# One pair of VectorE operations makes the block exponents of two tiles of h instead of one

## The chip, the cores and the metric

The kernel runs on one core of a Trainium2 chip. The metric is the device time in microseconds (us), from the first to the last instruction and what lies around them; the profile's span covers the instructions alone. Three runs of the kernel before have a median of 321.7 us (321.41 to 323.46).

## The reference

A post-norm transformer block on x of shape [2, 2048, 256]: linear attention, then an MLP whose two linear layers take block-quantised operands.

```
x = layernorm(x + attn(x))        # q, k, v = x Wqkv^T + b, scaled; q, k -> elu + 1
                                  # y = q * cumsum(k v) / clip(sum(q * cumsum(k)), 1e-3); y Wproj^T + b
x = layernorm(x + ffn(x))         # h = gelu(bq(x) bq(w_fc)^T + b_fc); bq(h) bq(w_proj)^T + b_proj

bq(v): in each block of 32 along the last axis
    e = floor(log2(max |v|));  scale = 2^(e - 3);  q = round(v / scale) * scale
```

The hidden layer h has 1024 columns, so each token has 32 blocks, each with a power of two of its own.

## The kernel before

**Tiling.** The 4096 tokens are cut into 8 chunks of 512; the chunks of the two sequences alternate. A chunk is 4 tiles of 128 tokens (tokens on the partitions), t = 0 to 3. Of a chunk the attention, the first layer norm, the up projection with gelu (h, four tiles of [128, 1024]), the quantisation of h, the down projection and the second layer norm are computed.

**Staging.** A step of the loop works on three chunks at once: A has its attention begun, B its attention ended, its first norm made and its up projection begun, and C has the rest of its MLP done. There is a written-out start, then 6 steps (a loop of 3 rounds, two steps in each), then a written-out tail for chunks 6 and 7. Each engine has a queue that it works through strictly in the order of the program text; the order of `step` in each engine's block sets the order of work. Engines wait for each other by semaphore counts; a waiting instruction holds up all that stands behind it on its engine.

**Quantising a tile of h.** Six operations on three engines:
1. VectorE takes the maximum of each block (`h_exponents`, line 718, `h_amax`), once both gelu halves of the tile are there (`s_h`).
2. VectorE masks the exponent bits of the maxima, which is the power of two (`powers`, line 621, `h_pow`).
3. VectorE makes the grid factor from it (`powers`, line 624, `h_inv`) and counts `s_hinv`.
4. GpSimd multiplies h with the factor into float16, which rounds (`round_h`, line 326, `h_round`; `h_round` has two buffers).
5. VectorE multiplies back with the power (`quantise_h`, line 629 in `times_power`, `hq`).
6. TensorE transposes `hq` (`transpose_hq`, line 957), ScalarE copies it from PSUM (`copy_hT`, line 446), TensorE does the down projection (`down`, line 964), VectorE adds the residual (`residual_2`, line 730).

The same `powers` serves the weights (lines 633 to 640) and x (`x_exponents`, line 706).

**Orders around the change.** VectorE's `step` ends with `h_exponents(B, 0)`, two `attention_out` (line 682, `y`), `h_exponents(B, 1)`, `quantise_h(B, 0)`. The next step, in which this chunk is C, begins with `h_exponents(C, 2)`, `residual_1(B, 0)` (line 686, `r1`), `quantise_h(C, 1)`, `h_exponents(C, 3)`, `residual_1(B, 1)`, `mean_var_1(B)`. GpSimd's `step` ends with `round_h(B, 0)`, `round_h(B, 1)`; the next begins with `round_h(C, 2)`, `scale_shift_1(B)` (lines 311 and 313), `round_h(C, 3)`. TensorE's has, in this order, `transpose_rec` (line 919), `up(C, 2)`, `project_out(B, 0)` (line 932), `up(C, 3)`, `transpose_hq(C, 0)`, `project(A)` for k (line 900), `project_out(B, 1)`, `project(A)` for q, `down(C, 0)`.

In the tail, VectorE does `mean_var_1(7)`, `h_exponents(6, 2)`, `quantise_h(6, 1)`, `x_exponents(7)`, `quantise_h(6, 2)`, `residual_2(6, 0)`, `quantise_x(7)`, `residual_2(6, 1)`, `h_exponents(6, 3)`. TensorE can start `up(6, 3)` only after `transpose_hq(6, 1)` and `down(6, 0)`; ScalarE does `norm_1(7)`, `copy_hT(6, 1)` and then the gelu of (6, 3) at line 436. GpSimd's tail is `scale_shift_1(7)`, `round_h(6, 2)`, `round_x(7)` (line 317), `round_h(6, 3)`, `round_h(7, 0)`, `round_h(7, 1)`, `round_h(7, 2)`, `scale_shift_2(6)`, `round_h(7, 3)`, `scale_shift_2(7)`. ScalarE's `norm_2(6)` (line 455, `o_sb`) stands before `copy_hT(7, 1)`, and VectorE's `residual_2(7, 0)` waits for it.

Of the kernel before, what the change touches and what calls it, by code (L numbers as in the profile page):

```python
# [45 lines left out]
def wait(engine, sem, value):  # L46

    if isinstance(value, int) and value <= 0:
        return
    engine.wait_ge(sem, value)  # L50


def block_kernel(nc, x, Wqkv, bqkv, Wproj, bproj, scale, w_fc, b_fc, w_pr, b_pr, out):
# [3 lines left out]
    TILES = 4  # L57
# [4 lines left out]
    HC = HID // P  # L62
# [3 lines left out]
    XB = C // BLOCK_K  # L66
    HB = HID // BLOCK_K
# [7 lines left out]
    with ExitStack() as ctx:  # L75
        def sb(name, shape, dt=F32):
            return ctx.enter_context(nc.sbuf_tensor(name, shape, dt))
# [4 lines left out]
        def sem(name):  # L82
            return ctx.enter_context(nc.semaphore(name))
# [13 lines left out]
        w_amax = sb("w_amax", [P, 2, HC * XB])  # L97
        w_inv = sb("w_inv", [P, 2, HC * XB], BF16)
        w_pow = sb("w_pow", [P, 2, HC * XB, 2], BF16)
# [36 lines left out]
        x_amax = sb("x_amax", [P, TILES * XB])  # L136
        x_inv = sb("x_inv", [P, TILES * XB], BF16)
        x_pow = sb("x_pow", [P, TILES * XB, 2], BF16)
# [6 lines left out]
        h_amax = sb("h_amax", [P, TILES, HB])  # L145
        h_inv = sb("h_inv", [P, TILES, HB], BF16)
        h_pow = sb("h_pow", [P, TILES, HB, 2], BF16)
# [38 lines left out]
        s_w_amax, s_w_exp, s_w_inv, s_w_round, s_wq = sem("w_amax_done"), sem("w_exponent_done"), sem("w_grid_ready"), sem("w_rounded"), sem("w_quantised")  # L186
# [31 lines left out]
        s_xamax, s_xexp, s_xinv = sem("x_amax_done"), sem("x_exponent_done"), sem("x_grid_ready")  # L218
# [6 lines left out]
        s_hamax, s_hexp, s_hinv = sem("h_amax_done"), sem("h_exponent_done"), sem("h_grid_ready")  # L225
# [65 lines left out]
        def _(pool):  # L291
# [28 lines left out]
                                        ALU.mult).then_inc(s_xround, 1)  # L320

            def round_h(S, t):
                wait(pool, s_hinv, 4 * S + t + 1)
                if t >= 2:
                    wait(pool, s_hq, 4 * S + t - 1)
                nc.gpsimd.tensor_tensor(h_round[:, t % 2].rearrange("p (g j) -> p g j", j=BLOCK_K),  # L326
                                        h[:, t].rearrange("p (g j) -> p g j", j=BLOCK_K),
                                        h_inv[:, t].unsqueeze(2).broadcast_to([P, HB, BLOCK_K]),
                                        ALU.mult).then_inc(s_hround, 1)
# [258 lines left out]
        def _(dve):  # L588
# [25 lines left out]
                        dve.wait_ge(s_bsplit, 2 * r + 2)  # L614
                    src = b_rest

            def powers(amax, pow2, inv, groups, s_amax, s_pow, s_inv, n):

                top = amax.bitcast(U16).rearrange("p (g o) -> p g o", o=2)[:, :, 1:2]
                wait(dve, s_amax, n)  # L620
                nc.vector.tensor_scalar(pow2.bitcast(U16), top.broadcast_to([P, groups, 2]), EXPONENT_BITS, None,  # L621
                                        ALU.bitwise_and).then_inc(s_pow, 1)
                wait(dve, s_pow, n)
                nc.vector.tensor_scalar(inv.bitcast(U16), pow2.bitcast(U16)[:, :, 0], -1.0, float(TO_GRID),  # L624
                                        ALU.mult, ALU.add).then_inc(s_inv, 1)

            def times_power(dst, src, pow2, groups):
                pairs = BLOCK_K // 2
                return nc.vector.tensor_tensor(dst.rearrange("p (g j o) -> p g j o", j=pairs, o=2),  # L629
                                               src.rearrange("p (g j o) -> p g j o", j=pairs, o=2),  # L630
                                               pow2.unsqueeze(2).broadcast_to([P, groups, pairs, 2]), ALU.mult)

            def w_exponents(n):
                w, w_sem = ((w_fc_sb, s_wfc), (w_pr_sb, s_wpr))[n]
                w = w.rearrange("p e (g j) -> p (e g) j", j=BLOCK_K)
                dve.wait_ge(w_sem, 16)
                nc.vector.tensor_reduce(w_amax[:, n], w, AX_X, ALU.max, apply_absolute_value=True).then_inc(s_w_amax, 1)
                powers(w_amax[:, n], w_pow[:, n], w_inv[:, n], HC * XB, s_w_amax, s_w_exp, s_w_inv, n + 1)
                dve.wait_ge(s_w_inv, n + 1)
                nc.vector.tensor_scalar(w_pow[:, n], w_pow[:, n], PRODUCT_STEP, None, ALU.mult).then_inc(s_w_pow, 1)  # L640

# [64 lines left out]
            def x_exponents(S, b):  # L706
                wait(dve, s_x1, S + 1)
                nc.vector.tensor_reduce(x_amax[:, :], x1[:, b].rearrange("p t (g j) -> p (t g) j", j=BLOCK_K), AX_X,  # L708
                                        ALU.max, apply_absolute_value=True).then_inc(s_xamax, 1)
                powers(x_amax[:, :], x_pow[:, :, :], x_inv[:, :], TILES * XB, s_xamax, s_xexp, s_xinv, S + 1)  # L710

            def quantise_x(S):
                wait(dve, s_xround, S + 1)
# [2 lines left out]
            def h_exponents(S, t):  # L716
                wait(dve, s_h, 8 * S + 2 * t + 2)
                nc.vector.tensor_reduce(h_amax[:, t], h[:, t].rearrange("p (g j) -> p g j", j=BLOCK_K), AX_X,  # L718
                                        ALU.max, apply_absolute_value=True).then_inc(s_hamax, 1)
                powers(h_amax[:, t], h_pow[:, t], h_inv[:, t], HB, s_hamax, s_hexp, s_hinv, 4 * S + t + 1)  # L720

            def quantise_h(S, t):
                wait(dve, s_hround, 4 * S + t + 1)
                times_power(hq[:, t], h_round[:, t % 2], h_pow[:, t], HB).then_inc(s_hq, 1)

            def residual_2(S, b, t):
                if isinstance(S, int) and t == 0:
                    wait(dve, s_o, S)
                wait(dve, s_down, 4 * S + t + 1)
                nc.vector.tensor_tensor(r2[:, t], down_ps, x1[:, b, t], ALU.add).then_inc(s_r2, 1)  # L730

            def mean_var_1(n):
                mean_var(n, r1, stats1, mv1, negmean1, vareps1, s_r1, 2 * n + 2, s_st1, s_mv1, s_ve1)
# [3 lines left out]


            w_exponents(0)
            split_biases()  # L740
            feature(0, 1, 0, abank[0])
# [32 lines left out]
            attention_out(1, 0)  # L774
            attention_out(1, 1)
            h_exponents(0, 1)
            quantise_h(0, 0)

            def step(A, B, C):
                n, b = C  # L780
                h_exponents(n, 2)
                n, b = B
                residual_1(n, b, 0)
                n, b = C
                quantise_h(n, 1)
                h_exponents(n, 3)
                n, b = B
                residual_1(n, b, 1)
                mean_var_1(n)
                n, b = C  # L790
                residual_2(n, b, 0)
                n, b = A
                feature(n, 1, 0, abank[0])
                n, b = C
                quantise_h(n, 2)
                n, b = A
                feature(n, 0, 0, abank[1])
                multiply_kv(n, 0, abank[0])
                n, b = C
                residual_2(n, b, 1)  # L800
                n, b = A
                sum_k(n, b, 0)
                n, b = B
                x_exponents(n, b)
                n, b = C
                quantise_h(n, 3)
                n, b = A
                feature(n, 1, 1, abank[1])
                feature(n, 0, 1, abank[0])
                sum_k(n, b, 1)  # L810
                n, b = B
                quantise_x(n)
                n, b = C
                residual_2(n, b, 2)
                n, b = A
                multiply_kv(n, 1, abank[1])
                sum_kv(n, b, 0)
                n, b = C
                residual_2(n, b, 3)
                mean_var_2(n)  # L820
                n, b = A
                denominator(n)
                sum_kv(n, b, 1)
                n, b = B
                h_exponents(n, 0)
                n, b = A
                attention_out(n, 0)
                attention_out(n, 1)
                n, b = B
                h_exponents(n, 1)  # L830
                quantise_h(n, 0)

            run(dve, step)
# [4 lines left out]
            mean_var_1(7)  # L838
            h_exponents(6, 2)
            quantise_h(6, 1)  # L840
            x_exponents(7, 1)
            quantise_h(6, 2)
            residual_2(6, 0, 0)
            quantise_x(7)
            residual_2(6, 0, 1)
            h_exponents(6, 3)
            h_exponents(7, 0)
            quantise_h(6, 3)
            h_exponents(7, 1)
            residual_2(6, 0, 2)  # L850
            h_exponents(7, 2)
            residual_2(6, 0, 3)
# [1 line left out]
            mean_var_2(6)  # L854
            quantise_h(7, 1)
            h_exponents(7, 3)
            quantise_h(7, 2)
            residual_2(7, 1, 0)
            quantise_h(7, 3)
# [372 lines left out]
```

## Time and profile before

| | |
|---|---|
| median of 3 runs | 321.7 us (321.41 to 323.46) |
| the profiled execution: its own time | 321.13 us |
| its span, first to last instruction | 319.3 us |
| busy: TensorE (PE) | 263.4 us, 82% |
| busy: VectorE (DVE) | 255.4 us, 80%, 505 instructions |
| busy: ScalarE (ACT) | 169.1 us, 53% |
| busy: GpSimd (POOL) | 159.8 us, 50% |
| mean granted clock of TensorE | 0.951 |

Busy time counts an instruction from its start to its end, also while it is held up by something else; matmuls overlap, so TensorE's busy time is more than its arithmetic needs. In a timeline row stand the start, the time from the first instruction of the row to the end of its last, engine, line, operation, output and inputs with their shapes, how many instructions the row holds, and in brackets how long the engine sat idle before and what ended that. An instruction on VectorE can start a little before the end of the one ahead is recorded, so the distance between two starts is what an instruction costs its engine.

### The profile page before, as it was taken

To read this page: it belongs to the slowest core of one execution; us is meant where nothing else is said; L and a number is where in the kernel's file an instruction comes from. 1 tells how busy PE (TensorE), PEld (TensorE's weight loads), DVE (VectorE), ACT (ScalarE), POOL (GpSimd) and SP (SyncE) were. 2 spreads that over 40 slices of the span, in tenths; PEclk is the share of its full clock that TensorE was granted. 3 is DMA by queue.
4 is the path that set the end of the run, shared out by engine and by line. 5 is a ranking of instruction groups with operands and counts; after the bars stand their busy time and mean duration, and the time that the engine had idled before them with its cause. 6 is when DMAs were issued, how large, how long until landed. Compare 5 with 4: busy or idle time off the path is not lost.

```text
span 319.3 us, 4631 instructions
## 1 busy us (share of the span) xinstructions
PE 263.4 (82%) x1476; PEld 164.8 (52%) x1476; DVE 255.4 (80%) x505; ACT 169.1 (53%) x278; POOL 159.8 (50%) x113
## 2 busy tenths in 40 slices
PE   5858964599899998999899989998999898768570
PEld 4515632276547554756466545664566445544350
DVE  2477745838989998899889988998899889867942
ACT  0633414235564856585657555764577547345242
POOL 0035242526364836573556555754666465575621
PEclk9799989759999999999999999999999999979987
DMA  6900002000200210010100120011001000100011
GB/s 178 348 1 3 0 1 66 0 2 1 66 0 2 68 51 17 0 63 9 60 0 21 45 66 0 0 66 66 0 0 66 0 0 2 66 0 3 0 67 66
DMA packets 13548, 11.70 MB, mean 37 GB/s; under 512 B 3040, under 2 KB 13280, under 8 KB 13536
## 3 DMA queue, kind: packets, MB, share of 16 engines
q1 hardware_dynamic: 11904, 11.28, 10.9%
q10 hardware_dynamic: 1632, 0.27, 0.5%
q8 instruction: 6, 0.10, 0.1%
q14 instruction: 6, 0.05, 0.0%
HBM read 7.35 MB, written 4.19 MB: 36 GB/s over the span
## 4 chain that ended last, share of the span: by engine, by line
DVE 50%; PE 25%; issue 13%; ACT 4%; DMA 3%; POOL 3%; SPq 0%; DVEq 0%; ACTq 0%; POOLq 0%
PE abank L900 11%; DVE h_amax L718 10%; DVE stats L692 7%; PE dbank L964 4%; DVE kf L653 3%; DMA h<-in_L_ffn_w_fc_dram 3%; DVE kvsum L670 3%; DVE h_pow L621 3%; DVE r L730 3%; DVE r L686 3%; DVE ksum L665 2%; PE bbank L932 2%; DVE hq L629 2%; DVE x_amax L708 2%; DVE kv L660 2%
## 5 line engine op out<-in xcount | busy, mean ns | idle before, releaser
L900 PE MATMUL abank<-xT,WqkvT 128*128 128x512 f32 x192 | 95.0, 622 | 25.3 <-DVE kf L653 21.0
L326 POOL TENSOR_TENSOR h_round<-h,h_inv 128x1024 f16<-128x1024 f32 x32 | 64.6, 2019 | 18.8 <-DVE h_inv L624 17.5
L900 PEld LDWEIGHTS abank<-xT,WqkvT 128*128 128x128 f32 x192 | 34.6, 196 | 60.9 <-DVE kf L653 28.0
L436 ACT ACTIVATE h<-hbank 128x512 f32<-128x512 f32 x64 | 37.5, 597 | 34.6 <-PE hbank L950 34.3
L311 POOL TENSOR_TENSOR rstd<-vareps,minus_half 128x4 f32<-128x4 f32 x16 | 17.4, 1090 | 55.4 <-DVE vareps L704 55.4
L302 POOL TENSOR_TENSOR qk<-qf,ksum 128x512 f32<-128x512 f32 x16 | 23.8, 1488 | 34.9 <-DVE ksum L665 29.2
L718 DVE TENSOR_REDUCE h_amax<-h 128x32 f32<-128x1024 f32 x32 | 38.6, 1208 | 1.7 <-ACT h L436 1.7
L950 PE MATMUL hbank<-w_fcT,xqT 128*128 128x512 bf16 x128 | 39.6, 392 | 0.0
L430 ACT ACTIVATE expz<-abank,zbias_neg 128x512 f32<-128x512 f32 x32 | 22.0, 688 | 33.1 <-PE abank L900 33.1
L446 ACT COPY hT<-tbank 128x512 uint32<-128x512 uint32 x32 | 18.6, 581 | 31.2 <-PE tbank L957 31.2
L964 PE MATMUL dbank<-w_prT,hT 128*128 128x256 bf16 x256 | 34.9, 282 | 0.0
L932 PE MATMUL bbank<-WprojT,y 128*128 128x256 f32 x128 | 31.9, 380 | 0.0
L629 DVE TENSOR_TENSOR hq<-h_round,h_pow 128x1024 bf16<-128x1024 f16 x32 | 30.0, 938 | 0.3 <-POOL h_round L326 0.3
L964 PEld LDWEIGHTS dbank<-w_prT,hT 128*128 128x128 bf16 x256 | 25.7, 101 | 7.9 <-issue 4.0
L306 POOL TENSOR_TENSOR num<-qf,kvsum 128x512 f32<-128x512 f32 x16 | 20.4, 1272 | 18.7 <-DVE kvsum L670 18.2
L948 PE MATMUL hbank<-bias_rows,ones_k 128*128 128x512 bf16 x64 | 25.3, 395 | 1.7 <-ACT xqT L440 0.8
L957 PE MATMUL tbank<-ident,hq 128*128 128x128 bf16 x256 | 20.3, 224 | 7.2 <-DVE hq L629 6.5
L957 PEld LDWEIGHTS tbank<-ident,hq 128*128 128x128 bf16 x256 | 17.3, 100 | 17.4 <-issue 14.1
L932 PEld LDWEIGHTS bbank<-WprojT,y 128*128 128x128 f32 x128 | 21.8, 190 | 6.1 <-issue 2.3
L692 DVE BATCH_NORM_STATS2 stats<-r 128x6 f32<-128x256 f32 x64 | 22.5, 414 | 0.5
L455 ACT ACTIVATE x<-r,shift,rstd 128x256 f32<-128x256 f32 x32 | 16.6, 590 | 10.1 <-POOL shift L313 9.7
L653 DVE SCALAR_TENSOR_TENSOR qf<-abank,zbias,expz 128x512 f32<-128x512 f32 x16 | 12.0, 751 | 12.4 <-ACT expz L432 11.8
(90 smaller groups left out, 425.5 us busy)
## 6 DMA issues: line engine op xcount, KB each, us to landing
x_sb<-in_L_attn_x_dram SPq DMA_DIRECT2D x8, 512.0 KB, 3.6
out_dram<-o_sb SPq DMA_DIRECT2D x7, 512.0 KB, 2.9
h<-in_L_ffn_w_fc_dram SPq DMA_DIRECT2D x1, 1024.0 KB, 10.1
h<-in_L_ffn_w_proj_dram SPq DMA_DIRECT2D x1, 1024.0 KB, 11.4
Wqkv_sb<-in_L_attn_Wqkv_dram SPq DMA_DIRECT2D x1, 512.0 KB, 6.5
out_dram<-o_sb SPq DMA_DIRECT2D x4, 128.0 KB, 1.7
Wqkv_sb<-in_L_attn_Wqkv_dram SPq DMA_DIRECT2D x1, 256.0 KB, 6.9
Wproj_sb<-in_L_attn_Wproj_dram ACTq DMA_DIRECT2D x1, 256.0 KB, 7.5
```

Source lines behind the costliest of these rows:

```text
L302: nc.gpsimd.tensor_tensor(qk[:, c], qf[:, c], ksum[:, b, c], ALU.mult).then_inc(s_qk, 1)
L326: nc.gpsimd.tensor_tensor(h_round[:, t % 2].rearrange("p (g j) -> p g j", j=BLOCK_K), h[:, t].rearrange("p (g j) -> p g j", j=BLOCK_K), h_ ...
L436: nc.scalar.activation(h[:, t, half * HALF:(half + 1) * HALF], hbank[half][:, :], ACT.Gelu).then_inc(s_h, 1)
L629: return nc.vector.tensor_tensor(dst.rearrange("p (g j o) -> p g j o", j=pairs, o=2), src.rearrange("p (g j o) -> p g j o", j=pairs, o=2), ...
L692: last = nc.vector.bn_stats(stats[:, t], r[:, t])
L718: nc.vector.tensor_reduce(h_amax[:, t], h[:, t].rearrange("p (g j) -> p g j", j=BLOCK_K), AX_X, ALU.max, apply_absolute_value=True).then_i ...
L900: last = nc.tensor.matmul(ps[:, :], WqkvT[:, k, e * P:(e + 1) * P], xT[:, k], start=(k == 0), stop=(k == CC - 1))
L932: last = nc.tensor.matmul(dst, y[:, c, t * P:(t + 1) * P], WprojT[:, c], start=False, stop=(c == CC - 1))
L948: nc.tensor.matmul(hbank[half][:, :], ones_k[:, :], bias_rows[:, cols], start=True, stop=False)
L950: last = nc.tensor.matmul(hbank[half][:, :], xqT[:, c, t * P:(t + 1) * P], w_fcT[:, c, cols], start=False, stop=(c == CC - 1))
L957: last = nc.tensor.transpose(t16[:, c * P:(c + 1) * P], hq[:, t, c * P:(c + 1) * P], ident16[:, :])
L964: last = nc.tensor.matmul(down_ps, hT[:, t % 2, c], w_prT[:, c], start=False, stop=(c == HC - 1))
```

## The change

`h_exponents(S, t)` keeps the maxima alone. A new `h_powers(S, pair)` makes the powers and the factors of tiles 0 and 1, or 2 and 3, in one pair of operations over 64 blocks a partition in place of 32, once the second tile's maxima are there. `s_hinv` counts pairs, and `round_h` waits for the pair. In the tail, `h_exponents(6, 3)` moves ahead of `x_exponents(7)`. For x and the weights nothing changes.

```
             def round_h(S, t):
-                wait(pool, s_hinv, 4 * S + t + 1)
+                wait(pool, s_hinv, 2 * S + t // 2 + 1)
...
-            def powers(amax, pow2, inv, groups, s_amax, s_pow, s_inv, n):
+            def powers(amax, pow2, inv, groups, s_amax, n_amax, s_pow, s_inv, n):
...
-                wait(dve, s_amax, n)
+                wait(dve, s_amax, n_amax)
...
                 nc.vector.tensor_reduce(h_amax[:, t], ...).then_inc(s_hamax, 1)
-                powers(h_amax[:, t], h_pow[:, t], h_inv[:, t], HB, s_hamax, s_hexp, s_hinv, 4 * S + t + 1)
+
+            def h_powers(S, pair):
+
+                t = slice(2 * pair, 2 * pair + 2)
+                powers(h_amax[:, t].rearrange("p t g -> p (t g)"), h_pow[:, t].rearrange("p t g o -> p (t g) o"),
+                       h_inv[:, t].rearrange("p t g -> p (t g)"), 2 * HB, s_hamax, 4 * S + 2 * pair + 2, s_hexp, s_hinv, 2 * S + pair + 1)
...
(start)      h_exponents(0, 1)
+            h_powers(0, 0)
             quantise_h(0, 0)
(step)           quantise_h(n, 1)
                 h_exponents(n, 3)
+                h_powers(n, 1)
...
                 h_exponents(n, 1)
+                h_powers(n, 0)
                 quantise_h(n, 0)
(tail)       h_exponents(6, 2)
             quantise_h(6, 1)
+            h_exponents(6, 3)
+            h_powers(6, 1)
             x_exponents(7, 1)
             quantise_h(6, 2)
             residual_2(6, 0, 0)
             quantise_x(7)
             residual_2(6, 0, 1)
-            h_exponents(6, 3)
             h_exponents(7, 0)
             quantise_h(6, 3)
             h_exponents(7, 1)
+            h_powers(7, 0)
             residual_2(6, 0, 2)
             h_exponents(7, 2)
             residual_2(6, 0, 3)
...
             quantise_h(7, 1)
             h_exponents(7, 3)
+            h_powers(7, 1)
             quantise_h(7, 2)
```

## Rows read from the trace of the kernel before

**Rows 1.** The page, part 4: the chain that ended last, shares of the span.

```profile
DVE 50%; PE 25%; issue 13%; ACT 4%; DMA 3%; POOL 3%; SPq 0%; DVEq 0%; ACTq 0%; POOLq 0%
```

**Rows 2.** Timeline of VectorE, end of one step and start of the next.

```profile
203.81 1.20 DVE L718 TENSOR_REDUCE h_amax<-h 128x32 f32<-128x1024 f32 x1
205.03 0.26 DVE L621 TENSOR_SCALAR h_pow<-h_amax 128x64 uint16<-128x64 uint16 x1
205.33 0.18 DVE L624 TENSOR_SCALAR h_inv<-h_pow 128x32 uint16<-128x32 uint16 x1
205.42 1.28 DVE L682 TENSOR_TENSOR y<-num,bbank 128x512 f32<-128x512 f32 x2
...
208.19 0.68 DVE L629 TENSOR_TENSOR hq<-h_round,h_pow 128x1024 bf16<-128x1024 f16 x1
...
210.03 0.65 DVE L621 TENSOR_SCALAR h_pow<-h_amax 128x64 uint16<-128x64 uint16 x1
...
210.84 0.69 DVE L686 TENSOR_TENSOR r<-bbank,x_sb 128x512 f32<-128x512 f32 x1
211.45 2.06 DVE L629 TENSOR_TENSOR hq<-h_round,h_pow 128x1024 bf16<-128x1024 f16 x1
...
215.00 0.69 DVE L686 TENSOR_TENSOR r<-bbank,x_sb 128x512 f32<-128x512 f32 x1
```

**Rows 3.** Timeline of GpSimd over the same stretch and the rest of that step.

```profile
205.59 1.90 POOL L326 TENSOR_TENSOR h_round<-h,h_inv 128x1024 f16<-128x1024 f32 x1 [0.34 <-DVE h_inv L624]
208.35 2.28 POOL L326 TENSOR_TENSOR h_round<-h,h_inv 128x1024 f16<-128x1024 f32 x1 [0.86 <-DVE h_inv L624]
211.06 1.90 POOL L326 TENSOR_TENSOR h_round<-h,h_inv 128x1024 f16<-128x1024 f32 x1 [0.42 <-DVE h_inv L624]
...
219.11 0.51 POOL L313 TENSOR_TENSOR shift<-negmean,rstd 128x4 f32<-128x4 f32 x1
219.58 1.90 POOL L326 TENSOR_TENSOR h_round<-h,h_inv 128x1024 f16<-128x1024 f32 x1
```

**Rows 4.** Groups by line: the same two operations over 64 blocks (the weights').

```profile
L621 DVE TENSOR_SCALAR w_pow<-w_amax 128x128 uint16<-128x128 uint16 x2 | 0.5, 227 | 0.1
...
L624 DVE TENSOR_SCALAR w_inv<-w_pow 128x64 uint16<-128x64 uint16 x2 | 0.4, 195 | 0.1
```

**Rows 5.** Timeline of VectorE in the tail.

```profile
281.04 0.68 DVE L629 TENSOR_TENSOR hq<-h_round,h_pow 128x1024 bf16<-128x1024 f16 x1
...
287.18 0.69 DVE L629 TENSOR_TENSOR xq<-x_round,x_pow 128x1024 bf16<-128x1024 f16 x1 [1.46 <-POOL x_round L317]
...
291.51 1.22 DVE L718 TENSOR_REDUCE h_amax<-h 128x32 f32<-128x1024 f32 x1 [1.74 <-ACT h L436]
...
305.55 0.42 DVE L730 TENSOR_TENSOR r<-dbank,x 128x256 f32<-128x256 f32 x1 [1.12 <-ACT o_sb L455]
```

**Rows 6.** Timeline of GpSimd in the tail.

```profile
284.86 2.28 POOL L317 TENSOR_TENSOR x_round<-x,x_inv 128x1024 f16<-128x1024 f32 x1 [1.38 <-DVE x_inv L624]
```

**Rows 7.** Timeline of TensorE: start, a step, the tail.

```profile
20.46 3.70 PE L900 MATMUL abank<-xT,WqkvT 128*128 128x512 f32 x8 [3.73 <-DVE kf L653]
...
46.19 5.20 PE L900 MATMUL abank<-xT,WqkvT 128*128 128x512 f32 x8 [2.88 <-DVE kv L660]
...
210.09 0.61 PE L957 MATMUL tbank<-ident,hq 128*128 128x128 bf16 x8
...
213.39 1.03 PE L932 MATMUL bbank<-WprojT,y 128*128 128x256 f32 x4
...
272.51 0.27 PE L930 MATMUL bbank<-bias_rows,ones_k 128*128 128x256 bf16 x1 [1.83 <-DVE y L682]
```

**Rows 8.** Windows: stretch, busy times of the engines, granted clock, DMA share, GB/s.

```profile
47.00:48.00 1.00, 1.00 (x2) 0.34 (x1) 0.96 (x3) 0.00 (x0) 0.00 (x0) 0.50 0.00 0
```

**Rows 9.** Timeline of ScalarE in the tail.

```profile
285.53 1.25 ACT L436 ACTIVATE h<-hbank 128x512 f32<-128x512 f32 x2 [1.98 <-PE hbank L950]
...
303.44 2.07 ACT L455 ACTIVATE o_sb<-r,shift,rstd 128x256 f32<-128x256 f32 x4 [3.09 <-POOL shift L313]
```

More of the change, by code:

```diff
@@ L322, in round_h @@
             def round_h(S, t):
-                wait(pool, s_hinv, 4 * S + t + 1)
+                wait(pool, s_hinv, 2 * S + t // 2 + 1)
                 if t >= 2:
@@ L615, in split_biases, with powers @@
                     src = b_rest
-            def powers(amax, pow2, inv, groups, s_amax, s_pow, s_inv, n):
+            def powers(amax, pow2, inv, groups, s_amax, n_amax, s_pow, s_inv, n):
                 top = amax.bitcast(U16).rearrange("p (g o) -> p g o", o=2)[:, :, 1:2]
-                wait(dve, s_amax, n)
+                wait(dve, s_amax, n_amax)
                 nc.vector.tensor_scalar(pow2.bitcast(U16), top.broadcast_to([P, groups, 2]), EXPONENT_BITS, None,
@@ L637, in w_exponents @@
                 nc.vector.tensor_reduce(w_amax[:, n], w, AX_X, ALU.max, apply_absolute_value=True).then_inc(s_w_amax, 1)
-                powers(w_amax[:, n], w_pow[:, n], w_inv[:, n], HC * XB, s_w_amax, s_w_exp, s_w_inv, n + 1)
+                powers(w_amax[:, n], w_pow[:, n], w_inv[:, n], HC * XB, s_w_amax, n + 1, s_w_exp, s_w_inv, n + 1)
                 dve.wait_ge(s_w_inv, n + 1)
@@ L709, in x_exponents @@
                                         ALU.max, apply_absolute_value=True).then_inc(s_xamax, 1)
-                powers(x_amax[:, :], x_pow[:, :, :], x_inv[:, :], TILES * XB, s_xamax, s_xexp, s_xinv, S + 1)
+                powers(x_amax[:, :], x_pow[:, :, :], x_inv[:, :], TILES * XB, s_xamax, S + 1, s_xexp, s_xinv, S + 1)
             def quantise_x(S):
@@ L719, in h_exponents, with h_powers @@
                                         ALU.max, apply_absolute_value=True).then_inc(s_hamax, 1)
-                powers(h_amax[:, t], h_pow[:, t], h_inv[:, t], HB, s_hamax, s_hexp, s_hinv, 4 * S + t + 1)
+            def h_powers(S, pair):
+                t = slice(2 * pair, 2 * pair + 2)
+                powers(h_amax[:, t].rearrange("p t g -> p (t g)"), h_pow[:, t].rearrange("p t g o -> p (t g) o"),
+                       h_inv[:, t].rearrange("p t g -> p (t g)"), 2 * HB, s_hamax, 4 * S + 2 * pair + 2, s_hexp, s_hinv, 2 * S + pair + 1)
             def quantise_h(S, t):
@@ L776, in _ @@
             h_exponents(0, 1)
+            h_powers(0, 0)
             quantise_h(0, 0)
@@ L786, in step @@
                 h_exponents(n, 3)
+                h_powers(n, 1)
                 n, b = B
@@ L830, in step @@
                 h_exponents(n, 1)
+                h_powers(n, 0)
                 quantise_h(n, 0)
@@ L840, in _ @@
             quantise_h(6, 1)
+            h_exponents(6, 3)
+            h_powers(6, 1)
             x_exponents(7, 1)
@@ L845, in _ @@
             residual_2(6, 0, 1)
-            h_exponents(6, 3)
             h_exponents(7, 0)
@@ L849, in _ @@
             h_exponents(7, 1)
+            h_powers(7, 0)
             residual_2(6, 0, 2)
@@ L856, in _ @@
             h_exponents(7, 3)
+            h_powers(7, 1)
             quantise_h(7, 2)
```

## The prediction

> **What bounds the kernel now.** I read the chain of waits first: half of the chain that ended last lies on VectorE, a quarter on TensorE [rows 1]. So VectorE's order of work is the path, and a saved VectorE instruction can count; so can a new stop on it. Then VectorE's timeline where a step ends and the next begins [rows 2]: from the maxima of tile 0 (203.81) to `residual_1(B, 1)` (215.00) it works 11.19 us with no idle time. Third, GpSimd's timeline beside it [rows 3], since the roundings are what the change releases later. The two together show a fact that the list of waits does not. `hq` at 211.45 takes 2.06 us where the same operation takes 0.68 at 208.19, and it ends (213.51) 0.55 after the rounding that runs from 211.06 to 212.96; `h_pow` at 210.03 takes 0.65 instead of 0.26 or less and ends at 210.68, just after the rounding that ends at 210.63. So these VectorE operations do not run beside a rounding on GpSimd: they finish as if they had started 0.13 to 0.15 us before its end. The other way about, the rounding at 208.35 begins under an `hq` and takes 2.28 in place of 1.90.
>
> **What the change removes and adds in a step.** Removed: the pair of tile 0, 0.39 us (205.03 to 205.42), and the pair of tile 2, 0.81 (210.03 to 210.84), long because of GpSimd. The two pairs that stay have twice the blocks; the weights' rows have that size, 227 and 195 ns [rows 4], about 0.05 more a pair than the small ones. Also gone is the 1.38 us for which `hq` of tile 1 is held up (2.06 - 0.68), because GpSimd will have no rounding of tile 2 to do yet. In all 0.39 + 0.81 + 1.38 - 0.10 = 2.48 us less.
>
> Added: a stop. `quantise_h(B, 0)` stands right behind the pair now, and GpSimd gets the factor of tile 0 only with that pair. Before, the rounding of tile 0 ran under `y` and the maxima of tile 1. From rows: GpSimd starts 0.08 after the factor's end (205.51 to 205.59), rounds for 1.90, and VectorE starts 0.04 after a rounding ends (287.14 on GpSimd, 287.18 on VectorE [rows 5, 6]); with the 0.08 by which the next instruction would have overlapped, 2.1 us. That alone leaves VectorE 0.4 us ahead a step.
>
> **Who gets through first.** GpSimd's `round_h(B, 1)` is released by the same pair, so it follows tile 0's rounding without a gap. In the one row in a step where GpSimd's next rounding is free to go, it starts 0.04 *before* the end of its predecessor (219.11 + 0.51 = 219.62, next 219.58 [rows 3]). VectorE's `hq` of tile 0 can start only 0.04 *after* that end. So GpSimd is 0.08 ahead, and `hq` is then held up by a second rounding, 1.90 more. No row shows this very meeting; the bounds are 0 (VectorE gets in) and 1.7 (held up until 0.14 before the end of the second rounding). I take the upper one, because in all rows the operation that started later is the one that is held. The Trainium skill, SBUF — State Buffer, section "Who interferes with whom", has a rule that speaks against this change: a VectorE operation with both inputs in SBUF and a GpSimd operation that reads SBUF exclude each other for a whole instruction, and the order of issue decides. By that rule the held case is right; against it the other sum below would hold.
>
> The step then, in the time of [rows 2]. Pair: the maxima of tile 1 end and the pair starts 0.39 earlier, the factor is ready at 207.93; roundings 208.01 to 209.91 and 209.87 to 211.77; `hq` ends at 211.63 + 0.68 = 212.31. TensorE starts `transpose_hq` 0.15 later, 212.46, against 210.09 [rows 7]: 2.37 later. Behind it on TensorE stand `project(A)` and `project_out(B, 1)`, whose last matmuls ran from 213.39 to 214.42, and `residual_1(B, 1)` needs them: 214.42 + 0.04 + 2.37 = 216.83 against 215.00. VectorE by itself would be there at 216.3, so TensorE sets it: **+1.83 us a step**. Later in the step TensorE's own slack takes up nothing more. The collision is met at the end of the start and of 5 steps before the tail: 6 x 1.83 = 11.0, and 0.4 for the first, where `y` waits for TensorE and does not come earlier: +11.4.
>
> **The clock.** TensorE idles 2.7 us a step before that transpose (209.7, the 210.09 of its transpose less 0.39, since `y` comes 0.39 earlier, to 212.46). The matmuls after 2.88 idle ran at the lower of the two levels, granted clock 0.50, 1.2 GHz [rows 8], and 8 of them took 5.20 where 8 took 3.70 after an idle time of 3.73; after 1.83 of idle the clock stayed up [rows 7]. So a fall costs 1.5, and it will not come each time. Bounds 0 and 6 x 1.5 = 9.0; I take half, +4.5.
>
> **The tail.** `h_exponents(6, 3)` now stands ahead of `x_exponents(7)`, and needs the gelu that ran at 285.53 to 286.78 [rows 9]. TensorE gets to that `up` only after `quantise_h(6, 1)`, at 281.04 before [rows 5], so VectorE stops for some 5 us with nothing else allowed. In the held case `quantise_h(6, 1)` starts at 282.6 (+1.54), the gelu ends at 288.3, maxima and pair take 1.24 + 0.37 to 290.0, then the maxima of x; x's power is held by `round_h(6, 2)` (290.1 to 292.0); `round_x(7)` runs 292.4 to 294.7, its 2.28 as in [rows 6]; `round_h(6, 3)` follows without a gap and holds `quantise_x(7)`, which acts as if it began at 296.4 against 287.18: **+9.2**. All of chunk 7's MLP hangs on it (the maxima at 291.51 waited for gelu). Next, `round_h(7, 2)` and behind it in GpSimd's queue `scale_shift_2(6)` now wait for `h_powers(7, 1)`. Counted from the maxima of (7, 0): `hq` of (7, 0) held until 7.9, `mean_var_2(6)` to 10.0, `hq` of (7, 1), maxima of (7, 3) and pair to 12.3, rounding to 14.3, the shift at 15.6, and `norm_2(6)` for 2.07 as in [rows 9] to 17.7. `residual_2(7, 0)` waits for it: 17.8 against 14.04 (305.55 - 291.51): **+3.75**. TensorE idles over 4 us twice more; at half clock the next work costs by a step's price between 0 and 3.0; I take 2.4.
>
> **Sum.** 11.4 + 4.5 + 9.2 + 3.75 + 2.4 = 31.2. The profiled execution took 321.13 (span 319.3 and 1.8 around it), 0.6 below the median 321.7: **352 us**. Own range, from the clock bounds: 345 to 358.
>
> **Rivals.**
> *VectorE gets in first.* The stop is then 2.1. VectorE alone gains 0.39 a step, but TensorE's transpose starts 0.68 late and `residual_1(B, 1)` lands at 215.14, +0.14: 6 x 0.14 + 0.4 = +1.2. Tail: `quantise_x` at 293.0, +5.8; the second part +2.35; clock +2.4. Sum +11.8: 333 us. For it: 0.08 us is small. Against it: the rows above.
> *Faster: the saved VectorE time outweighs the stop.* Its place is the loop, its price the 2.48 freed against the stop; it decides where the stop is under 2.48 and TensorE takes the late transpose up in its slack: -0.39 x 6 = -2.3. The tail's four small pairs give -1.3 if the 5 us stop there is covered: 317.5. Against it: nothing stands before `h_exponents(6, 3)` that could cover.
> *Loop even, tail mostly hidden:* 319 to 325.
>
> **How the numbers follow.** Forecast 0.70; VectorE first 0.22; even 0.05; faster 0.03. The range must hold 8 in 10, so it reaches down into the second case: 330 to 358. A measurement here can tell about 1%: faster 0.03, within 1% 0.04, slower 0.93.
>
> **What would show it.** In the changed profile: in each step one `hq` of about 2.4 us, recorded from just after the first rounding to the end of the second; two roundings back to back; `hq` of tile 1 at 0.68; TensorE idle 2.7 us before `tbank` released by `hq`, and slow matmuls behind some of these. In the tail: VectorE idle about 5 us before `h_amax`, released by gelu; `norm_2(6)` some 4 us later against the maxima of (7, 0). If `hq` of tile 0 starts late but takes 0.68 and the second rounding takes 2.3 or more, the second case is right. If VectorE's idle time before `h_amax` is short, the tail's term falls.

## The result, and where the time went

The changed kernel takes 351.92 us (median of 4 runs, 350.17 to 353.10) against 321.73 (4 runs, 321.41 to 323.46): ratio 1.091, 95% interval 1.086 to 1.097. The forecast was 352 us, range 330 to 358.

| profiled execution | before | after |
|---|---|---|
| own time / span, us | 321.13 / 319.3 | 350.17 / 348.0 |
| VectorE busy, instructions | 255.4 (80%), 505 | 253.7 (73%), 473 |
| GpSimd busy | 159.8 | 155.4 |
| mean granted clock | 0.951 | 0.915 |

VectorE has 32 instructions less and is hardly less busy, over a span 28.7 us longer. The chain of waits after (part 4 of the page) answers to [rows 1]:

```profile
DVE 36%; PE 32%; issue 12%; POOL 11%; ACT 4%; DMA 3%; SPq 0%; POOLq 0%; ACTq 0%; DVEq 0%
```

VectorE's share has gone from 50% to 36% and GpSimd's from 3% to 11%: the roundings are on the path now. VectorE's timeline after, the same stretch as [rows 2]:

```profile
212.91 1.19 DVE L718 TENSOR_REDUCE h_amax<-h 128x32 f32<-128x1024 f32 x1
214.02 1.27 DVE L682 TENSOR_TENSOR y<-num,bbank 128x512 f32<-128x512 f32 x2
215.21 1.21 DVE L718 TENSOR_REDUCE h_amax<-h 128x32 f32<-128x1024 f32 x1
216.46 0.23 DVE L621 TENSOR_SCALAR h_pow<-h_amax 128x128 uint16<-128x128 uint16 x1
216.72 0.20 DVE L624 TENSOR_SCALAR h_inv<-h_pow 128x64 uint16<-128x64 uint16 x1
218.93 2.37 DVE L629 TENSOR_TENSOR hq<-h_round,h_pow 128x1024 bf16<-128x1024 f16 x1 [2.01 <-POOL h_round L326]
...
222.95 0.67 DVE L629 TENSOR_TENSOR hq<-h_round,h_pow 128x1024 bf16<-128x1024 f16 x1
...
225.74 0.69 DVE L686 TENSOR_TENSOR r<-bbank,x_sb 128x512 f32<-128x512 f32 x1 [0.49 <-PE bbank L943]
```

The stop of 2.01 us stands in the row of `hq`, and then `hq` itself takes 2.37, while `hq` of tile 1, held in [rows 2], is down to 0.67. From the maxima of tile 0 to `residual_1(B, 1)` it is 12.83 us, 11.19 before: +1.64. GpSimd's row after, beside [rows 3], holds both roundings, 3.76 us from 216.99 to 220.75 with no gap; below it is the second of them by itself:

```profile
216.99 3.76 POOL L326 TENSOR_TENSOR h_round<-h,h_inv 128x1024 f16<-128x1024 f32 x2 [2.65 <-DVE h_inv L624]
...
218.85 1.90 POOL L326 TENSOR_TENSOR h_round<-h,h_inv 128x1024 f16<-128x1024 f32 x1
```

The first rounding ended at 218.89. The second started at 218.85, `hq` at 218.93, 0.08 behind it, and `hq` ran to 221.30, 0.55 behind the end of the second: the offset that the held `hq` showed before. TensorE after, beside [rows 7], idles 2.51 us in front of the transpose and hands the delay on to `project_out(B, 1)`:

```profile
221.35 0.62 PE L968 MATMUL tbank<-ident,hq 128*128 128x128 bf16 x8 [2.51 <-DVE hq L629]
...
224.67 1.03 PE L943 MATMUL bbank<-WprojT,y 128*128 128x256 f32 x4
```

Once a step VectorE's statistics of `mean_var_1` are a mark from which steps can be counted. First before, then after (first step, three in a row, and the tail):

```profile
84.38 1.41 DVE L692 BATCH_NORM_STATS2 stats<-r 128x6 f32<-128x256 f32 x4
...
277.33 1.41 DVE L692 BATCH_NORM_STATS2 stats<-r 128x6 f32<-128x256 f32 x4
```

```profile
86.69 1.41 DVE L692 BATCH_NORM_STATS2 stats<-r 128x6 f32<-128x256 f32 x4
...
121.23 1.40 DVE L692 BATCH_NORM_STATS2 stats<-r 128x6 f32<-128x256 f32 x4
...
155.73 1.41 DVE L692 BATCH_NORM_STATS2 stats<-r 128x6 f32<-128x256 f32 x4
...
191.95 1.41 DVE L692 BATCH_NORM_STATS2 stats<-r 128x6 f32<-128x256 f32 x4
...
291.58 1.40 DVE L692 BATCH_NORM_STATS2 stats<-r 128x6 f32<-128x256 f32 x4
```

Five steps of the loop took 32.8 each before; after, four take 34.5 and one 36.2. From the first mark to the tail's it is 204.89 us against 192.95, +11.9; from there to the end of the span 56.42 against 41.97, +14.45; the start has +2.3, a share that is uncertain, as the first mark moves by more than that between kernels with the same start. In the step of 36.2 the granted clock is at its lower level (1.2 GHz) for 3 us, as this window shows (columns as in [rows 8]):

```profile
187.00:188.00 1.00, 1.00 (x3) 0.31 (x2) 1.00 (x2) 0.00 (x0) 0.00 (x0) 0.50 0.00 0
```

The tail after: VectorE, then GpSimd.

```profile
294.85 0.68 DVE L629 TENSOR_TENSOR hq<-h_round,h_pow 128x1024 bf16<-128x1024 f16 x1
300.76 1.22 DVE L718 TENSOR_REDUCE h_amax<-h 128x32 f32<-128x1024 f32 x1 [5.22 <-ACT h L436]
...
303.63 0.87 DVE L621 TENSOR_SCALAR x_pow<-x_amax 128x64 uint16<-128x64 uint16 x1
...
307.10 2.38 DVE L629 TENSOR_TENSOR xq<-x_round,x_pow 128x1024 bf16<-128x1024 f16 x1 [1.46 <-POOL x_round L317]
...
314.79 1.22 DVE L718 TENSOR_REDUCE h_amax<-h 128x32 f32<-128x1024 f32 x1 [4.98 <-ACT h L436]
...
332.85 0.42 DVE L735 TENSOR_TENSOR r<-dbank,x 128x256 f32<-128x256 f32 x1 [2.66 <-ACT o_sb L455]
```

```profile
302.55 1.90 POOL L326 TENSOR_TENSOR h_round<-h,h_inv 128x1024 f16<-128x1024 f32 x1 [6.96 <-DVE h_inv L624]
304.79 2.27 POOL L317 TENSOR_TENSOR x_round<-x,x_inv 128x1024 f16<-128x1024 f32 x1 [0.35 <-DVE x_inv L624]
307.03 1.90 POOL L326 TENSOR_TENSOR h_round<-h,h_inv 128x1024 f16<-128x1024 f32 x1
```

The stop ahead of the maxima of (6, 3) is 5.22 us. x's power (0.87) is held by the rounding of (6, 2), and `xq` (2.38) by that of (6, 3), which starts 0.03 before `x_round` ends. From the maxima of (7, 0) to `residual_2(7, 0)` it is 18.06, 14.04 before [rows 5].

### The profile page after: what moved, and what is told of

It is laid out like the page before. It is cut to its first block, busy times and chain, and to the rows that moved or that the text cites. A ratio compares the mean times of both kernels' runs of the same rounds, so it can differ in the third digit from the quotient of the medians.

```text
span 348.0 us, 4568 instructions
## 1 busy us (share of the span) xinstructions
PE 273.2 (79%) x1460; PEld 168.2 (48%) x1476; DVE 253.7 (73%) x473; ACT 168.7 (48%) x278; POOL 155.4 (45%) x113
## 4 chain that ended last, share of the span: by engine, by line
DVE 36%; PE 32%; issue 12%; POOL 11%; ACT 4%; DMA 3%; SPq 0%; POOLq 0%; ACTq 0%; DVEq 0%
PE abank L911 13%; DVE stats L692 6%; DVE hq L629 5%; PE dbank L975 5%; POOL h_round L326 5%; PE bbank L943 4%; DVE kvsum L670 3%; DVE kf L653 3%; DMA h<-in_L_ffn_w_fc_dram 3%; PE tbank L968 3%; POOL num L306 3%; DVE ksum L665 2%; POOL rstd L311 2%; DVE r L735 2%; DVE x_amax L708 2%
## 5 line engine op out<-in xcount | busy, mean ns | idle before, releaser
L911 PE MATMUL abank<-xT,WqkvT 128*128 128x512 f32 x192 | 99.4, 647 | 19.0 <-DVE kf L653 14.8
L326 POOL TENSOR_TENSOR h_round<-h,h_inv 128x1024 f16<-128x1024 f32 x32 | 60.5, 1900 | 70.5 <-DVE h_inv L624 70.5
L911 PEld LDWEIGHTS abank<-xT,WqkvT 128*128 128x128 f32 x192 | 35.7, 202 | 57.1 <-issue 27.5
L629 DVE TENSOR_TENSOR hq<-h_round,h_pow 128x1024 bf16<-128x1024 f16 x32 | 34.4, 1073 | 16.1 <-POOL h_round L326 16.1
L961 PE MATMUL hbank<-w_fcT,xqT 128*128 128x512 bf16 x128 | 41.4, 408 | 3.0 <-ACT xqT L440 1.1
L975 PE MATMUL dbank<-w_prT,hT 128*128 128x256 bf16 x256 | 36.7, 291 | 0.3 <-ACT hT L446 0.3
L975 PEld LDWEIGHTS dbank<-w_prT,hT 128*128 128x128 bf16 x256 | 26.5, 104 | 8.8 <-issue 4.0
L735 DVE TENSOR_TENSOR r<-dbank,x 128x256 f32<-128x256 f32 x32 | 13.4, 419 | 11.1 <-PE dbank L975 8.4
```

Source lines behind the costliest of these rows:

```text
L911: last = nc.tensor.matmul(ps[:, :], WqkvT[:, k, e * P:(e + 1) * P], xT[:, k], start=(k == 0), stop=(k == CC - 1))
L961: last = nc.tensor.matmul(hbank[half][:, :], xqT[:, c, t * P:(t + 1) * P], w_fcT[:, c, cols], start=False, stop=(c == CC - 1))
L975: last = nc.tensor.matmul(down_ps, hT[:, t % 2, c], w_prT[:, c], start=False, stop=(c == HC - 1))
```

## The experiments

The tables below give medians, ratios to the pooled runs of the kernel before (their median lies between 322.28 and 322.72 us, by how many there were), and from each profile the stretch from the first mark to the tail's ("loop", 192.95 before, 204.89 after) and from there to the end ("tail", 41.97 and 56.42). The start is left out: with equal code the first mark lay at 84.38 in the kernel before and at 87.53 in one of the kernels below.

**1. Is it the second rounding that holds hq?** GpSimd's rounding of tile 1 waits for `hq` of tile 0:

```
             def round_h(S, t):
                 ...
+                if t == 1:
+                    wait(pool, s_hq, 4 * S + 1)
```

> The changed kernel, but GpSimd's rounding of tile 1 also waits until VectorE has quantised tile 0, so that no second rounding can hold hq of tile 0 up. Theory (VectorE waits 2.0 us for the first rounding and is then held by the second one through the shared port): every hq takes 0.68 us, the loop comes to +0.1 to +0.3 us a step over the kernel before, the tail keeps most of its loss: 337 to 341 us. Rival (the loss of the loop is the wait for the first rounding alone, the long hq hides nothing): 348 us or more.

Measured: 338.43 us, ratio 1.051 (1.045 to 1.057); loop 193.06, tail 56.44. VectorE still stops 2.0 us, but `hq` takes 0.69:

```profile
80.34 0.69 DVE L631 TENSOR_TENSOR hq<-h_round,h_pow 128x1024 bf16<-128x1024 f16 x1 [2.02 <-POOL h_round L328]
```

The loop is back to 0.1 us of the loop before. The wait for the first rounding costs what the change saves; the 1.7 us a step are the second rounding's. The tail keeps all of its loss.

**2. What decides who gets in?** Memsets on GpSimd between the two roundings, with no wait added: one of 128x4, two of 128x4, one of 128x128.

```
             def round_h(S, t):
+                if t == 1:
+                    nc.gpsimd.memset(scratch[:, :], 0.0)      # once or twice, or 128x128
                 wait(pool, s_hinv, 2 * S + t // 2 + 1)
```

> The changed kernel with one memset of 128x4 (some 0.1 us, reads nothing) on GpSimd between the roundings of tiles 0 and 1; no wait is added. Theory (the order of issue decides, and GpSimd is ahead by only 0.08 us): VectorE's hq of tile 0 now gets in first, takes 0.68 us, the second rounding takes 2.3 or more; 337 to 341 us, like the kernel with the added wait. Rival (GpSimd keeps the port over a queue of its instructions, or wins whatever the order): hq still takes 2.3 us or more, time as the changed kernel, 350 to 353.

> With one small memset between the two roundings the second one still started 0.01 us before the first one's end (0.04 before without it), so GpSimd stayed ahead of VectorE, which starts 0.03 to 0.04 behind that end, and hq took 2.4 us. Here there are two memsets of 128x4. The second rounding should start some 0.05 behind the end, within 0.02 of VectorE. Theory (the order of issue decides): either hq is held as before, or it is let in; this lies at the edge. Rival (GpSimd keeps the port whatever the order): held, 350 to 353 us.

> The changed kernel with one longer memset, 128x128 (0.2 us elsewhere in the trace), between the two roundings. The second rounding should start 0.1 us or more behind the first one's end, VectorE 0.03 to 0.04 behind it. Theory (the order of issue decides): hq takes 0.68 us in every step, the second rounding 2.3 or more, and the time is that of the kernel with the added wait, 337 to 341 us. Rival (GpSimd keeps the port from one of its instructions to the next): hq 2.4 us or more, 350 to 353.

| between the roundings | second rounding starts, against the first one's end | hq starts, against it | hq takes | median, us | ratio |
|---|---|---|---|---|---|
| nothing (the change, 4 runs) | 0.04 before | 0.04 after | 2.37 | 351.92 | 1.091 (1.086 to 1.097) |
| 128x4 (4 runs) | 0.01 before | 0.03 after | 2.41 | 352.49 | 1.094 (1.086 to 1.101) |
| 128x4 twice (2 runs) | 0.03 after | 0.04 after | 2.44 | 353.76 | 1.099 (1.091 to 1.108) |
| 128x128 (4 runs) | 0.10 after | 0.03 after | 0.69 | 338.70 | 1.051 (1.044 to 1.058) |

The first expectation of these missed: the small memset was taken up in the end of the rounding before it and moved the next by 0.03 us alone, so VectorE was still second. The other two bracket the point. GpSimd's rows and VectorE's, with two memsets:

```profile
78.75 1.90 POOL L330 TENSOR_TENSOR h_round<-h,h_inv 128x1024 f16<-128x1024 f32 x1 [4.59 <-DVE h_inv L628]
80.59 0.10 POOL L325 MEMSET scratch<- 128x4 f32 x1
80.63 0.10 POOL L326 MEMSET scratch<- 128x4 f32 x1
80.68 1.90 POOL L330 TENSOR_TENSOR h_round<-h,h_inv 128x1024 f16<-128x1024 f32 x1
```

```profile
80.69 2.44 DVE L633 TENSOR_TENSOR hq<-h_round,h_pow 128x1024 bf16<-128x1024 f16 x1 [2.01 <-POOL h_round L330]
```

and with the longer one:

```profile
79.10 1.90 POOL L329 TENSOR_TENSOR h_round<-h,h_inv 128x1024 f16<-128x1024 f32 x1 [4.83 <-DVE h_inv L627]
80.94 0.20 POOL L325 MEMSET scratch<- 128x128 f32 x1
81.10 2.39 POOL L329 TENSOR_TENSOR h_round<-h,h_inv 128x1024 f16<-128x1024 f32 x1
```

```profile
81.03 0.69 DVE L632 TENSOR_TENSOR hq<-h_round,h_pow 128x1024 bf16<-128x1024 f16 x1 [2.02 <-POOL h_round L329]
```

At 0.01 us behind, `hq` is held for 1.76; at 0.07 ahead it goes first, and the rounding takes 2.39 in place of 1.90. The same holds in each of the seven places of start and loop in these traces. One filler instruction of 0.2 us makes the kernel 13 us faster. The rival that GpSimd stays ahead whatever the order is refuted.

**3. Loop and tail apart.** Once the pairs in start and loop with the tail as before, once the loop as before with the changed tail:

```
 # tail as before, loop changed:            # loop as before, tail changed:
             h_exponents(6, 2)                 h_exponents(n, t)
+            tile_powers(6, 2)                +tile_powers(n, t)   # in start and loop
             quantise_h(6, 1)
-            h_exponents(6, 3)
-            h_powers(6, 1)
             x_exponents(7, 1)
             ...
+            h_exponents(6, 3)
+            tile_powers(6, 3)
             ...
```

> The changed kernel in start and loop (pairs), the tail as before: order of before and a pair of operations for each tile. Theory: the tail's part of the loss, 9.1 + 4.0 and some 3 of clock, is gone, the loop's 12 to 14 stays: 333 to 337 us. Rival (the tail only passes on what the loop lost): 345 or more.

> The kernel before in start and loop (powers tile by tile), the tail of the changed kernel. Theory: the tail alone costs 7.3 for the stop ahead of the maxima of (6, 3) and the held xq, 4.0 for norm_2(6), 3 of clock: 334 to 337 us. Together with the kernel that has only the loop changed it should add up to the whole change, less some 1.8 for hq of (6, 0). Rival (only the loop matters): 322 to 325.

| | median | ratio | loop | tail |
|---|---|---|---|---|
| loop changed, tail before | 336.10 | 1.041 (1.035 to 1.048) | 204.86 | 42.01 |
| loop before, tail changed | 338.25 | 1.049 (1.044 to 1.055) | 192.92 | 56.75 |

Each half keeps its own loss to 0.4 us: in the profiles the changed loop adds 11.9 and the changed tail 14.8, together 26.7 against 26.4 in the whole change. The medians lie 13.4 and 15.6 above the 322.66 of the kernel before, 29.0 together, against 30.2 for the whole change. The overlap of 1.8 for `hq` of (6, 0) that the expectation allowed for doesn't show: that hold-up lies in the last step of the changed loop, with either tail. The second came 1.2 us above its expectation, and its start was a slow one (87.53 at the first mark).

**4. The clock.** Extra transposes keep TensorE at work:

```
+            def fill(count, ps=t16):
+                for _ in range(count):
+                    nc.tensor.transpose(ps[:, 0:P], ident16[:, :], ident16[:, :])
 (step)          wait(pe, s_xqT, n + 1)
+                fill(32)
                 transpose_hq(n, 0)
 (tail)      fill(24 to 80) at five places
```

> The changed kernel with extra bf16 transposes on TensorE whose result nobody uses, ahead of the places where it idles 2 us or more: 32 ahead of transpose_hq(C, 0) in each step, 24 to 80 at five places of the tail. Theory (the lower clock after idle time costs 1.7 in a step where it falls, and 3.0 in the tail): granted clock 1.00 there, 345 to 348 us. Rival (the clock's fall is hidden behind VectorE): 350 to 352.

Measured: 345.37 us, ratio 1.072 (1.066 to 1.077); loop 203.22, tail 51.27. Granted clock 1.00 in the tail's windows from 288 to 336. In the loop it gives back 1.67, the one fall in the profile of the changed kernel. In the tail it gives back 5.15. Of this 1.75 lie between the end of `xq` and the maxima of (7, 0), and 1.33 behind `residual_2(7, 0)`: these are the two stretches in which the changed kernel had lost 1.67 and 1.40 against the kernel before. Another 1.58 lie ahead of the maxima of (6, 3), where the stop shrinks from 5.22 to 3.65. The kernel before ran at the lower clock in that place as well (0.50 from 282 to 284, TensorE behind an idle time of 3.56), so they are no loss of the change. The last 0.51 lie between the maxima of (7, 0) and `residual_2(7, 0)`.

**5. The second rounding and the changed tail both gone.** Pairs in start and loop, tail as before, and the wait of experiment 1, first everywhere and then not for chunk 7:

```
+                if t == 1 and not (isinstance(S, int) and S == 7):
+                    wait(pool, s_hq, 4 * S + 1)
```

> Pairs in start and loop, the tail as before, and GpSimd's rounding of tile 1 waits until VectorE has quantised tile 0. Theory: both causes are gone; the loop is +0.14 a step, the time 321 to 324 us, no better than the kernel before although VectorE has 14 pairs of small operations less. Rival (the removed operations do shorten the path once nothing holds hq): 315 to 319.

> Pairs in start and loop, the tail as before, GpSimd's rounding of tile 1 waits until VectorE has quantised tile 0, but not for chunk 7 (the earlier kernel had that wait in the tail too, which held the roundings of chunk 7 back by 2 us). Theory: with both causes gone the time is within 1% of the kernel before, 321 to 324 us. Rival (a third cause of loss): 326 or more.

The first gave 325.89 us, above its expectation, with runs from 318.83 to 327.29, too scattered for a ratio; its profile has 193.15 for the loop and 45.38 for the tail. The second, without the wait for chunk 7, gave 323.28, ratio 1.004 (1.000 to 1.008), loop 193.06, tail 42.33. So that wait had cost the 3 us of the tail. Of the loss no more than 0.5 us is left over, and nothing of a gain has come: VectorE has 26 instructions less than in the kernel before (13 pairs, not the 14 of the expectation) and the time is the same. VectorE's stop of 2.0 us for the first rounding is still in each step and takes up what was freed, and `residual_1(B, 1)` starts 0.04 after the last matmul of `project_out(B, 1)`, which TensorE reaches no earlier than before.

**6. Where a gain lies.** Pairs only where nothing waits for them at once (tiles 2 and 3, in the loop), and, apart from it, the kernel before with one wait more on GpSimd:

```
 # pair of tiles 2 and 3 only               # no pairs, the kernel before with
                 h_exponents(n, 1)           def round_h(S, t):
+                tile_powers(n, 1)          +    if t == 2 and not isinstance(S, int):
                 ...                        +        wait(pool, s_hq, 4 * S + t)
                 h_exponents(n, 3)
                 h_powers(n, 1)
```

> Only the powers of tiles 2 and 3 are made together, in the loop; tiles 0 and 1 and the whole tail as before. Theory: no stop arises, since quantise_h(C, 2) stands far behind the pair; hq of tile 1 is no longer held by the rounding of tile 2 (2.06 to 0.68), and residual_1(B, 1) comes 0.54 earlier a step, when TensorE's project_out lets it: 318 to 319.5 us. Rival (all of VectorE's 2.1 us a step come through): 308 to 311. Rival (nothing comes through): 321 to 322.

> The kernel before, with no pairs: in the loop GpSimd's rounding of tile 2 waits until VectorE has quantised tile 1, nothing else. Theory: the gain of the kernel that pairs tiles 2 and 3 is that of the hold-up of hq, not of the operations saved, so this one gets the same: 318 to 319.5 us, within 0.3% of that kernel. Rival (the saved operations make the gain): this one stays at 321 to 322.

| | median | ratio | loop | tail |
|---|---|---|---|---|
| pair of tiles 2 and 3 | 319.89 | 0.990 (0.984 to 0.996) | 190.56 | 42.35 |
| no pair, rounding of tile 2 waits | 319.78 | 0.990 (0.986 to 0.994) | 190.55 | 41.98 |

Both are some 1% faster than the kernel before, with medians 0.3 to 0.4 us above the range expected, and equal to 0.1 us in the loop. So the gain needs no saved instruction: to free `hq` is enough. VectorE in the kernel with the pair:

```profile
210.46 0.69 DVE L638 TENSOR_TENSOR hq<-h_round,h_pow 128x1024 bf16<-128x1024 f16 x1
211.65 1.22 DVE L727 TENSOR_REDUCE h_amax<-h 128x32 f32<-128x1024 f32 x1 [0.50 <-ACT h L445]
...
214.25 0.69 DVE L695 TENSOR_TENSOR r<-bbank,x_sb 128x512 f32<-128x512 f32 x1 [0.89 <-PE bbank L960]
```

`hq` of tile 1 is down from 2.06 to 0.69, and 1.39 us of what was freed turn up as two new waits, 0.50 for the gelu and 0.89 for `project_out`. And in the kernel without the pair:

```profile
210.01 0.68 DVE L631 TENSOR_TENSOR hq<-h_round,h_pow 128x1024 bf16<-128x1024 f16 x1
...
213.01 0.69 DVE L688 TENSOR_TENSOR r<-bbank,x_sb 128x512 f32<-128x512 f32 x1
```

From the maxima of tile 0 to `residual_1(B, 1)` it is 10.66 us with the pair (203.59 to 214.25) and 10.65 without (202.36 to 213.01), and in both `residual_1` starts 0.03 to 0.04 after the last matmul of `project_out(B, 1)`. TensorE's order sets that point in both, and it caps what VectorE can gain. Whether the saved instructions would have done as much with `hq` still held was not run.

**7. Taking the new wait away.** On TensorE `project_out(B, 1)` goes ahead of k's projection:

```
                 transpose_hq(n, 0)
+                n, b = B
+                wait(pe, s_y, 2 * n + 2)
+                project_out(n, 1)
                 n, b = A
                 wait(pe, s_xT, 2 * n + 1)
                 project(n, 1, 0, abank[0])
-                n, b = B
-                wait(pe, s_y, 2 * n + 2)
-                project_out(n, 1)
```

> The powers of tiles 2 and 3 together in the loop, tiles 0 and 1 and the tail as before, and on TensorE project_out(B, 1) ahead of project(A) for k instead of behind it. In the trace of the kernel with the pair alone VectorE idles 0.9 us a step before residual_1(B, 1), which waits for project_out, and 0.5 for gelu. Theory: residual_1 comes up to 1.0 earlier, k's features and kv are then limited by ScalarE and TensorE, so 0.3 to 0.8 a step comes through: 314 to 318 us. Rival (k's projection 2 us later delays the features by as much as is gained): 319 to 322.

Measured: 319.28 us, ratio 0.992 (0.989 to 0.995), a step 32.28 us against 32.35 without the swap: the rival's number. But the traces show other reasons than the rival's. Counted from the maxima of tile 0, VectorE's statistics start 1.00 us earlier than without the swap, and k's features (`kf`) are not late but 0.24 earlier. They gain no more because `residual_2`, ahead of them, now waits 0.69 for TensorE's `down`. The rest goes in a new hold-up. With the statistics earlier, GpSimd's `scale_shift_1` and the rounding of tile 3 behind it are earlier too; that rounding now starts ahead of `hq` of tile 2 and holds it, 2.08 us in place of 0.68, and q's features come 0.53 later than without the swap. VectorE, then GpSimd:

```profile
216.66 0.42 DVE L747 TENSOR_TENSOR r<-dbank,x 128x256 f32<-128x256 f32 x1 [0.69 <-PE dbank L992]
...
217.66 2.08 DVE L638 TENSOR_TENSOR hq<-h_round,h_pow 128x1024 bf16<-128x1024 f16 x1
```

```profile
217.29 1.91 POOL L335 TENSOR_TENSOR h_round<-h,h_inv 128x1024 f16<-128x1024 f32 x1
```

What the swap gives with this hold-up taken away was not run.

## Why the prediction was right, term by term

The mechanism was right in every place, and the number is in part luck. The terms are summed against the profiled execution of the kernel before, so they answer to the profiled execution of the changed one, and there they are 2.5 us too high: its span is 28.7 us longer, not 31.2. The forecast of 352 meets the median of 351.92 because the median lies 1.75 above the profiled execution, which no term had. The terms:

| term | predicted | measured |
|---|---|---|
| start and five steps of the loop | 11.4 | 10.8 (2.3 for the start, uncertain, + 5 x 1.69) |
| lower clock in the loop | 4.5 (3 of 6 steps) | 1.7 (1 of 6) |
| tail up to `quantise_x` | 9.2 | 9.14 |
| maxima of (7, 0) to `residual_2(7, 0)` | 3.75 | 4.02 |
| lower clock in the tail | 2.4 | 3.0 (what is left: 1.67 + 1.40 in two stretches) |
| sum | 31.2 | 28.7 |

The last step's own loss is in the third row, as in the prediction. The last clock term is the rest of the span once the others are taken off; experiment 4, which gives both of its stretches back, shows that it is the clock.

- **Who gets through first.** This was the one choice between 352 and 333, and no row of before showed it. It came out as argued from a lead of 0.08 us. Experiments 1 and 2 show that the order decides: 338 us once VectorE is first, in either of two ways. The rule of the Trainium skill (SBUF — State Buffer, "Who interferes with whom"), that the order of issue decides and the later one waits for the whole instruction, agrees with both sides of the bracket.
- **The step.** 1.69 was measured, 1.83 predicted. Of the difference 0.11 is that `y`, with no small pair ahead of it, starts 1.11 us after the maxima (212.91 to 214.02); I had let it start 1.22 after, where the pair used to start.
- **"It will not come each time", half of the steps.** This term was mis-sized, 1.7 in place of 4.5. TensorE's idle time is 2.4 to 2.5 us, not the 2.7 that I worked out, and the clock fell behind one of the six. How many fall is not fixed: the kernel with two memsets, with the same hold-up, has two such steps in its loop (36.3 us each). The price of a fall, 1.5, was about right (1.67 given back in experiment 4).
- **The tail.** The stop (5.22 against "some 5", both with TensorE at the lower clock), the held power of x, the held `xq` (2.38) and the late `norm_2(6)` all came where they were put; the kernel of experiment 3 that has the loop of before shows that they are the tail's own.
- **VectorE first, 333.** The mechanism of this rival came true in experiment 1, at 338. Of the 5 us between, 4 lie in the tail. There `xq` is held all the same (2.37 in the kernel with the wait, where the rounding of (6, 3) follows `x_round` without a gap), which its sum left out, 1.8. `residual_2(7, 0)` comes 3.9 later against the maxima of (7, 0), not 2.35, and the clock costs 3.1, not 2.4. The rest lies ahead of the first mark (86.20 against 84.38), where equal code differs by more.
- **Faster.** Its first condition held once the hold-up was gone: the stop (2.01) is under the 2.48 us freed. No gain came of it: with the changed tail gone as well, the time is 1.004 of before, and `residual_1(B, 1)` still waits for TensorE (experiment 5). And where a gain exists it doesn't need the pairs (experiment 6).

The profiled execution was the shortest of the four. Why the others take up to 2.9 us more stays open, as they have no trace. A fall of the clock in another step or two would do it in time, but the mean granted clocks of the four (0.915, 0.915, 0.920 and 0.915, the slowest last) don't show it.

## What to carry to other kernels

Merging small operations moves a release later: price what stood between the first operand's being ready and its use, since here that distance hid a whole rounding. When operations of two engines can't run side by side, ask of each wait that ends on one of them what the other has ready to go at the same instant; here a lead of less than 0.1 us decided over a whole instruction. And a held instruction can be cured by one wait, or by a short filler, on the engine that holds it: here that gave 13 us back in the changed kernel, and a wait gave 2.5 us in the kernel before, while the saved instructions showed no gain of their own.

## What was not expected of the hardware

- A GpSimd memset of 128x4 (0.10 us in the trace) between two long operations delays the second by only 0.03 us; two by 0.07; one of 128x128 (0.20 us) by 0.14.
- VectorE's small power operation is held by a rounding too, though it has one input: 0.87 us for x's in the tail, against 0.20 where nothing runs beside it. (The prediction had this already, from the 0.65 in [rows 2].)
- The start of the program, with equal code, ends up to 3.1 us apart (84.38 at the first mark in the kernel before, 87.53 in the one of experiment 3 with the same start), more than a step's loss. Part of it is TensorE's clock: from 50 to 80 us the mean granted clock is 0.77 in the one and 0.61 in the other. Differences of a microsecond are better read between two marks of a trace than from the whole time.
